# The last batch of a Mamba and mixture-of-experts layer: six loads moved to ScalarE's queue, a looser rule in the planner, and the last batch's side work laid out anew

## The reference

```
xz = hidden @ in_proj.T                      # x: 1024 channels, z (the gate): 1024 channels
x  = silu(conv4(x) + conv_b)                 # causal, per channel
dt, B, C = split(x @ x_proj.T)               # 32, 16, 16
delta = softplus(dt @ dt_proj.T + dt_b)
h[t] = h[t-1] * exp(delta[t] * A) + delta[t] * B[t] * x[t]     # 16 states per channel
y[t] = sum_n h[t, n] * C[t, n] + D * x[t]
x1   = layernorm(hidden + (y * silu(z)) @ out_proj.T)
top2 of x1 @ gate.T -> weights by softmax
x2   = layernorm(x1 + sum over the 2 experts of weight * (x1 @ expert.T + bias))
```

## Time and profile before

| | us |
|---|---|
| median of 3 runs | 2286.59 |
| the runs | 2284.71, 2302.08, 2286.59 |
| span of the profiled execution | 2281.1 |

### The profile page before, as it was taken

The page is one execution under the profiler, slowest core; times in us unless marked ns, Lnnn a source line. Parts: engine busy times, 40 slices in busy tenths (PEclk is TensorE's granted clock), DMA queues, the critical chain, the costliest instruction groups (busy, mean ns, idle before and its releaser), DMA issues.

```text
span 2281.1 us, 30428 instructions
## 1 busy us (share of the span) xinstructions
PE 2037.1 (89%) x8624; PEld 1201.8 (53%) x8624; DVE 1983.3 (87%) x2191; ACT 1660.2 (73%) x3074; POOL 1850.8 (81%) x1505
## 2 busy tenths in 40 slices
PE   8896779789898989999899989999799998879998
PEld 3444455455554645545555555645455555545543
DVE  5899999899999989898899899899898988889911
ACT  5758858677598856988588876989579785666534
POOL 2959999589898979889898889899898897686503
PEclk9896879889999999999999999999999999769999
DMA  5513143158854776557754687556855575466875
GB/s 169 180 47 92 38 139 111 51 172 252 278 129 143 241 255 180 143 168 257 256 152 119 201 266 234 129 180 216 284 149 141 180 252 209 123 209 215 278 278 120
DMA packets 222085, 412.79 MB, mean 181 GB/s; under 512 B 29880, under 2 KB 36152, under 8 KB 221920
## 3 DMA queue, kind: packets, MB, share of 16 engines
q1 hardware_dynamic: 180448, 322.36, 42.1%
q0 software_dynamic: 20496, 57.16, 12.3%
q10 hardware_dynamic: 20976, 31.33, 4.1%
HBM read 299.37 MB, written 85.72 MB: 169 GB/s over the span
## 4 chain that ended last, share of the span: by engine, by line
POOL 25%; PE 10%; issue 9%; DMA 7%; DVE 7%; ACT 3%; SPq 1%; ACTq 0%; DVEq 0%; POOLq 0%
POOL hst L1704 12%; PE bank L1137 8%; POOL first_dbu L1704 4%; DMA y<-scaled 2%; DVE hst L1755 2%; DVE y L1744 2%; POOL delta L1675 2%; POOL u L1678 2%; DVE hst L1920 1%; DMA Bbc<-b_scratch 1%; POOL ysb L1630 1%; DVE u L1775 1%; PE hTp L1153 1%; POOL zs L1649 1%; ACT dA L1563 1%
## 5 line engine op out<-in xcount | busy, mean ns | idle before, releaser
L1563 ACT ACTIVATE dA<-delta,negA 128x512 f32<-128x512 f32 (+1 forms) x1146 | 712.2, 636 | 307.9 <-DVE hst L1755 248.2
L1704 POOL TENSOR_TENSOR hst<-u,Bbc 128x512 f32<-128x512 f32 x666 | 870.7, 1412 | 42.3 <-PE hTp L1153 26.9
L1755 DVE TENSOR_TENSOR_SCAN hst<-dA,hst 128x512 f32<-128x512 f32 x672 | 791.0, 1211 | 50.9 <-ACT dA L1563 46.9
L1153 PEld LDWEIGHTS hTp<-ident,hst 128*128 128x128 f32 x4096 | 498.3, 149 | 325.6 <-issue 140.4
L1153 PE MATMUL hTp<-ident,hst 128*128 128x128 f32 x4096 | 560.1, 288 | 106.0 <-DVE hst L1755 33.7
L1744 DVE SCALAR_TENSOR_TENSOR y<-hTp,Ct,y 128x1024 f32<-128x1024 f32 x463 | 587.1, 1268 | 69.4 <-PE hTp L1153 54.9
L1704 POOL TENSOR_TENSOR first_dbu<-u,Bbc 128x512 f32<-128x512 f32 x222 | 292.9, 1393 | 42.0 <-DVE hits L1836 29.2
L1755 DVE TENSOR_TENSOR_SCAN hst<-dA,first_dbu 128x512 f32<-128x512 f32 x224 | 263.3, 1210 | 9.5 <-ACT dA L1563 7.0
L1137 PE MATMUL bank<-wslot,hidT 128*128 128x512 f32 x512 | 244.3, 610 | 10.4 <-ACT zs L1459 5.0
L1137 PE MATMUL bank<-wslot,tokT 128*128 128x512 f32 x480 | 234.6, 617 | 9.7 <-ACT tokT L1474 9.7
L1137 PE MATMUL bank<-delta,tokT 128*128 128x512 f32 x480 | 220.8, 593 | 0.0
(11 more groups left out here) (187 smaller groups left out, 2874.8 us busy)
## 6 DMA issues: line engine op xcount, KB each, us to landing
wslot<-in_w_expT SPq DMA_DIRECT2D x90, 1024.0 KB, 6.5
Bbc<-b_scratch SPq DMA_DIRECT2D x113, 256.0 KB, 3.5
wslot<-in_w_inT SPq DMA_DIRECT2D x26, 1024.0 KB, 6.1
y<-scaled POOLq DMA_DIRECT2D x49, 512.0 KB, 5.3
zs<-sorted_tokens ACTq DMA_DIRECT2D x91, 256.0 KB, 5.1
sorted_results<-ysb SPq DMA_DIRECT2D x90, 256.0 KB, 6.2
res<-in_w_expT SPq DMA_DIRECT2D x18, 1024.0 KB, 6.9
gate_scratch<-zs SPq DMA_DIRECT2D x64, 256.0 KB, 2.1
```

Source lines behind the costliest of these rows:

```text
L1153: mm = nc.tensor.transpose(hTp[q % 2][:, tok(j)], hst[n % 2][:, j, start:start + P], ident[:, :])
L1563: nc.scalar.activation(decay_of(step, halved), delta[w.odd][:, j, cols], ACT.Exp, scale=negA[:, j, n:n + 1]).then_inc(exp_done, 1)
L1704: nc.gpsimd.tensor_tensor(dbu_row(n, j), u[w.odd][:, j, :], Bbc[n % 2][:, :], ALU.mult).then_inc(dbu_done, 1)
L1755: nc.vector.tensor_tensor_scan(hst[n % 2][:, j, :], dA[j % 2][:, :], dbu_row(n, j), 0.0, ALU.mult, ALU.add).then_inc(scan_done, 1)
```

## The change

Five things are edited:

1. `szE` (gate rows) and new pieces `WoE` (the two weight blocks) are issued by ACT in the last batch, with the waits that they need. SP no longer issues them there.
2. The costs and delays of these pieces in `tasks` follow. `out` there waits for `WoE`.
3. `may_start`: a state part may be followed by more than two turned pieces, if the one before the last in the same row has been copied out by ACT. On the chip `turned_piece` waits for that (`turned_taken`, `count - 2`). This stands in `plan`, which lays out every kind of batch.
4. In the last batch ACT copies out turned pieces in the order in which they were turned.
5. The urgencies and the pace of `SEG_EPI` are new numbers. Those of `SEG_TWO` and `SEG_FULL` are as they were.

```diff
-        "gy": [] if alone else [("pool", 1.4, [(("sz", k), "sp", 5), (("szE", k // HALF), "sp", 8), (("row", 2 * (t + 1) if t is not None else 0), "dve", 0.1)])],
+        "gy": [] if alone else [("pool", 1.4, [(("sz", k), "sp", 5), (("szE", k // HALF), "act", 6), (("row", 2 * (t + 1) if t is not None else 0), "dve", 0.1)])],
...
-        "out": [("pe", mm, [(("yT", 2 * k + 1), "act", 0.1), (("load_Wo",), "sp", 11)]), ("dve", 0.7, [(x, "pe", 0.1), (("load_res", k), "sp", 6)])],
+        "out": [("pe", mm, [(("yT", 2 * k + 1), "act", 0.1), (("load_Wo",), "sp", 11), (("WoE",), "act", 8)]), ("dve", 0.7, [(x, "pe", 0.1), (("load_res", k), "sp", 6)])],
...
-        "szE": [("sp", 0.5, [])],
+        "szE": [("act", 0.35, [])],
+        "WoE": [("act", 0.7, [])],
...
             row = row_of("pe")
-            return len([y for r, y, _ in rows["pe"] if r == row and y[0] in TURNED]) < 2 and added.get(row, 1e9) + 0.1 <= now
+            here = [y for r, y, _ in rows["pe"] if r == row and y[0] in TURNED]
+            return added.get(row, 1e9) + 0.1 <= now and (len(here) < 2 or ended(here[-2], "act", 0.1))
...
             for x, cost, after in first:
+                if halved and e == "act" and x in turns and not all(ended(y, "act") for y in turns[:turns.index(x)]):
+                    continue
...
-SEG_EPI = Segment(by_urgency({"lz": 66977, "L0": -107229, "ld": 67022, "oe": -16774, "of": -17404, "ln": 50444, "sc": 47088, "wt": 31041, "we": 72523, "w2": 27267, "ww": 8736, "nz": -20788, "bi": -50819, "L1": -158950, "EE": 5557, "EF": 148016, "h0": 63625, "h1": 20853, "h2": -58415, "h3": 13355, "hl": -11051, "hd": -8221, "m5": -193015, "m6": 13327, "hm": -96262}), 0.15,
+SEG_EPI = Segment(by_urgency({"lz": -14, "L0": -106, "lr": 72, "oe": 116, "of": -111, "ln": -46, "sc": 76, "wt": -52, "we": -117, "w2": -173, "ww": 150, "nz": -5, "bi": 72, "L1": 12, "EE": 77, "EF": 121, "h0": 49, "h1": 120, "h2": -40, "h3": 117, "hl": 146, "hd": 117, "m5": 126, "m6": -14, "hm": 119}), 2,
...
-        self.half = {x: sum(self.turned_at[y] == self.turned_at[x] for y in turns[:k]) for x, k in self.turned.items()}
+        self.nth = {x: sum(self.turned_at[y] == self.turned_at[x] for y in turns[:k]) for x, k in self.turned.items()}
...
-        return 1 - self.seg.part_at[self.seg.turned_at[piece]] % 2, self.seg.half[piece], self.turned_base + (k + 1)
+        return 1 - self.seg.part_at[self.seg.turned_at[piece]] % 2, self.seg.nth[piece] % 2, self.turned_base + (k + 1)
+
+    def in_row(self, piece):
+
+        return self.seg.nth[piece]
...
-                if not w.seg.steps and w.seg.turned[x] > 1:
+                if not w.seg.steps and w.seg.turned[x] > 1 or w.seg.steps and w.in_row(x) > 1:
                     pe.wait_ge(turned_taken, count - 2)
...
+                elif name == "szE":
+                    t = x[1]
+                    if t == 0:
+                        act.wait_ge(delta_ready, w.b * ND + ND)
+                        for k in range(2):
+                            act.wait_ge(z_stored[k], w.b * (16 * NT))
+                    elif t == PAIR:
+                        act.wait_ge(dbu_done, w.b * (NS * ND))
+                    act.dma_start(early_z(t, 0, HALF), z_dram[w.e, tok(t), :].rearrange("p (k n) -> p k n", k=HALF)).then_inc(early_in[t], 16)
+                elif name == "WoE":
+                    act.wait_ge(exp_done, w.b * (NS * ND))
+                    for h in range(HALF):
+                        s = w.weights(("Wo", h))[0]
+                        act.dma_start(slot_of(w, s), block_src(("Wo", h))).then_inc(w_loaded[s], 16)
```

20 lines of the change are left out of this document (5 added, 15 removed).

## The result

The changed kernel takes **2446.3 us** (median of 4 runs, 2435.0 to 2449.4) where the kernel before took 2285.7 in the same session (2280.7 to 2302.1): **1.068 times as long, interval 1.064 to 1.072**. The prediction was 2336 us in a range of 2306 to 2372. The sign was right and the size three times too small.

What follows compares the result with a forecast made beforehand. The prediction took handovers between engines, none full, to bound the kernel. Five full batches +50, batch 1 +1 and the last batch -2 made +49 us on 2286.6: 2336 us, range 2306 to 2372.

Steps and rivals of the forecast that it cites:

- Which plans change, and that full batches carry it: The rule of `may_start` reorders whole-step batches too; five full batches were to add +50 us (+22 to +88).
- So I cost each eight steps by the engine that has most to do there: Full batches: summing the fullest engine's load per eight steps, 254.7 us before and 262.1 now, 7.4 us longer each.
- the 5 us named: Sign in full batches: the fifth sixteen-step window would be 5 us or more shorter than 49.8.
- the 7.7 us by which the account fell short: Full batch before the change: loads summed to 254.7 us against 262.4 measured; the prediction called this a fair account.
- I take 0.6 for each, 3 us: Five rows with three or four turned pieces: each waits 0.6 us for ACT's copy, 3 us a batch (0 to 5).
- My sign for being wrong upward: At rows with extra turned pieces: the forecast is wrong upward if waits for copies exceed 1 us each.
- waits at the turned pieces pile up: Rival, full batches: each of five rows costs a whole pair of steps, 3.4 us; +120 us, 2406 us; chance 0.08.
- The turn: Between batches: a second tile behind the turned pieces, 3.44 us at full rate; only the table's 2.5 us was counted.
- PE's clock: Shares on PE were costed at 0.86 us each; the forecast had no term for a slower clock.
- -2 us, from -8 to +5: Last batch: ACT's issue time, earlier gate rows, changed loads and a shorter end together were to give -2 us.
- Batch 1 (+1) and the tail: Batch 1 would get 1 us longer; the tail would keep the same order.

Runs made afterwards that it cites:

- e1_rule_full: Kernel before with only the turned-piece rule changed, in the batches of whole steps; last batch and its loads as before: 2420.7 us (ratio 1.060).
- e2_last_only: Changed kernel with the new rule only in the last batch; whole-step batches keep the order of before: 2299.2 us (ratio 1.0070).
- e4_split: Changed kernel with third and fourth turned pieces, and what follows them, moved to PE's next part row in full batches: 2403.6 us (ratio 1.051).
- e6_seam: Changed kernel with ACT's copy of tile moe9 moved behind the next batch's first two decays: 2437.8 us (ratio 1.065).
- e12_bulk_after: As e2_last_only, but ACT issues the last batch's gate rows and weights at step 8, behind token loads and B load: 2293.1 us (ratio 1.0030).
- e3_last_sp: As e2_last_only, but SP issues the early gate rows and out-projection weights at the start of the last batch: 2289.0 us (ratio 1.0020).
- e14_rule_from64: Kernel before with the new rule only from row 64 of the whole-step batches: 2301.9 us (ratio 1.0074).

## Why the prediction was wrong

- **Which plans change, and that full batches carry it: right.** By e1_rule_full and e2_last_only it is 138 of 154 us. That the kernel gets slower was right too, with a third of the size.
- **"So I cost each eight steps by the engine that has most to do there": this step failed.** It gave 7.4 us a batch. By sixteen steps the table said 0, +2.5, +3.0, +0.7, -7.6, +4.4, -1.6 and +6.4; measured in batch 3 were +6.0, +2.6, +3.4, **+12.1**, **-4.5**, +8.2, +2.5 and +3.9. Windows 2 and 3 came as said, and the fifth fell by nearly the 5 us named. The fourth, where the bound hardly moved, is the largest. The busy time of DVE in the five batches grew by 4 us and its idle time by 143, so the loads were right and the loss lay beside them. A bound by the fullest engine supposes that the handovers cost what they did before; in the new order they don't, and the 7.7 us by which the account fell short of the measured batch should have warned me.
- **"I take 0.6 for each, 3 us": mis-sized, and for the wrong mechanism.** DVE waits 4.9 + 3.4 + 3.3 + 3.5 = 15.1 us behind four of the five rows in batch 3, and not at all behind row 12. (The expectation for e4_split counted 16.9, with the 1.8 of row 22.) Splitting the rows gives back 43 / 5 = 8.6. The waits for copies fell from 5.6 to 2.9 us in that batch, and the 0.62 us of the earlier trace rows was not the one price in the trace, as I had written, but one of seven in the batch. Long rows hold up the part. My sign for being wrong upward, waits for copies over 1 us each, therefore looked at the wrong thing. The rival "waits at the turned pieces pile up" had 3.4 us for each, five rows and 2406 us, and was the nearest of all. I had argued it down with the planner's model of when a copy ends, which says nothing about how long the row becomes.
- **The turn: seen and set aside.** The prediction named the second tile and 3.44 us, and counted 2.5 inside the table. Measured at the turns into batches 3 to 6 are 6.41, 4.90, 5.06 and 3.36 us for the scan, where before the sum had waited 3.74, 2.26, 0.78 and 1.84. At the first of them PE's stretch of 8 shares takes 10.1 us, with the clock at 0.50 to 0.68 from 852 to 860 us. What was got back by moving the copy is 8 us in all; the sum's wait of 4.21 us in e6_seam hangs on PE's row.
- **PE's clock: missing.** All shares were costed at 0.86 us, the price at full clock; 148 us more of PE's busy time than before ran at 0.5. How much of that DVE paid is not shown.
- **The last batch, "-2 us, from -8 to +5": wrong, +16.** ScalarE's time to issue is not isolated by any run; e12_bulk_after, which keeps it, stands 4 us over e3_last_sp. (the earlier trace rows have 1.67 us for two issues together; the sum of 4.2 us has that right.) What the term left out is who is queued behind 4 MB on ScalarE's own queue: two token loads and a B load. The rule of the Trainium skill that I weighed ("DMA: Bandwidth & Descriptors", section "Issuing engines are not separate DMA queues": transfers of all queues interleave, only the time to issue is saved) I took for "the queue makes no difference"; e3_last_sp and e12_bulk_after put 10 and 6 us against that.
- **Batch 1 (+1) and the tail: right** (+0.6 and -1.2).

**What stays open.** The split leaves 95 us of the full batches' 147, nearly all as idle time of DVE, above all in steps 25 to 32 (+10.8 us over the five), 41 to 48 (+13.4), 57 to 64 (+23), 81 to 88 (+10.4), 113 to 120 (+11.2) and at the turn (+10.8). Most of it seems to hang on the order of steps 1 to 86: e14_rule_from64 has the old one there and four such rows per batch, and its full batches take 26 us more by the trace (the kernel 15 more, for its last batch is 10 us shorter). That is not proof, for its order after row 86 is not that of the changed kernel either. Which piece is to blame is not known. Three edits at the routing moved its waits to other engines. That the slow clock feeds back is not shown.

## What to carry to other kernels

Where several engines hand work round in a ring with two buffers, as here, a table of loads gave a floor for a batch in a new order and no forecast: ask of each row how long its longest uninterrupted stretch is, against how long the engine behind it can do without. Relaxing a scheduler's rule can change every plan that uses it, and the plan whose weights were chosen under the old rule came out worse here. Used in two rows only, which were then split, it gave 0.7%, and that not in the batches it reordered but in the batch behind them, mostly at its start, where the row before it had become short. So look for a gain or a loss beyond the stretch that was edited. Before a bulk load goes to another queue, list the small loads that this queue issues in the next 20 us.
